# A two-layer perceiver on one core: projections of the recurrence in another order with key lengths by token, and experts that gather their tokens

## The chip, the core and the metric

One Trainium2 chip, and of it one core. The metric is the device time of one execution in microseconds, as the median of several runs. The kernel before takes 994.61 us (median of 3 runs, 992.96 to 995.33).

## What is computed

Sixteen batches of 64 rows of 256 numbers (1024 tokens in all) go through six parts, each added to its input: attention on a context, a gated recurrence, batch attention with a mixture of experts, attention on the context again, latent attention, and adapters. The change touches two of them.

```python
# recurrence: H = 16 heads of HD = 16, T = 64 steps, B = 16 batches
q = silu(x @ Wq); k = silu(x @ Wk); v = x @ Wv
log_f = log_sigmoid(x @ Wf1 @ Wf2); gamma = -sigmoid(x @ Wgamma)
k = k / max(norm(k, over the 16 numbers of a head), 1e-12)
a = k * gamma * exp(log_f)
S = S * exp(log_f)                      # at each step
S = S + k * (a . S + v);  o = q . S
...
# experts: 8 of them, room for C = 256 tokens each
logits = x @ wr                         # x normalized
top1, top2                              # two experts of each token
loc1 = cumsum(m1, axis=0) - 1;  loc2 = cumsum(m2, axis=0) - 1 + m1.sum(0)
buf[top1, s1] = x; buf[top2, s2] = x    # those beyond C are dropped
y = (relu(buf @ w1 + b1) @ w2 + b2) * 0.8
out = g1 * y[top1, s1] + g2 * y[top2, s2]
```

## The kernel before, in words

The program is a row of stages. Each is a block in which all engines run their own lists of instructions, tied by semaphores, and a stage begins when the one before has ended on all engines. A token is a column (transposed tiles, `[128, 2, 1024]`) or a row (`[128, 8, 256]`). The order of the work on every engine is written out by hand. In the trace TensorE (PE) splits each fp32 matmul into two passes, so a product over both halves of the 256 inputs shows as x4.

**Projections of the recurrence** (`recurrence_projections_stage`, tiles p_ and rec_; L237 to L385). Layer norm and transposes give `xnT`. Then for each half c of the columns (512 of them) PE goes through the thirteen jobs of `RJOBS`, each into one of four PSUM banks, which ScalarE (ACT) empties: k0 and k1 (the keys, two halves m of the 256 outputs), low (96 rows that feed the gates), q0, q1, g0, f0 (gamma and the forget gate from 16 rows of low), v0, v1, g1, f1, gate0, gate1. ACT takes k and q twice, as they are and through a sigmoid. VectorE (DVE) forms the keys (L260) and their squares (L262), PE sums the squares over each head with the matrix `same_head`, which gives every one of the 16 rows of a head the same sum (L357), ACT takes the roots of 512 columns (L385, another function table than that of the sigmoids), and DVE bounds them (L266), inverts them (L270), scales the keys (L274) and forms `a` (L279). GpSimd (POOL) multiplies gamma by f twice (L309, L312) and makes the queries (L315). All this is done for c = 0 and then for c = 1.

**Recurrence** (`recurrence_stage`, tiles r_; L570 to L735). For each of 64 steps and both halves m PE adds the values (L679) and the decayed state summed over a head (L683), DVE updates the state (L624, L628, L635), POOL fades it and multiplies it by the query (L656, L662), and PE sums the output (L690). The values of four steps are spread to a diagonal by 16 copies on ACT into a ring of four buffers (`value_rows`, L724); the first three rings are filled at the start of the stage, and the first matmul waits for the first.

**Experts** (`moe_stage`, tiles m_; L1689 to L1990). For each of eight tiles of 128 tokens: layer norm (DVE, L122 to L142), transposes (PE, L149), gain and shift (ACT, L159), logits (PE, L1860). Pairs of tiles g go through `choices` (DVE, L1745 to L1756: the two best experts and their one-hot rows), `counts` (PE, L1869) and `first_places` (DVE, L1767 on: the place of each token in the list of its expert). `rows_of` (L1760 to L1762) turns a place into a row number of the buffer `expert_rows` in DRAM, and POOL scatters the tokens to it by an indirect DMA: sixteen of 128 rows each, eight for the first choices and eight for the second, which need the totals of all first choices (L1839). The buffer was zeroed in the stage before (L1586, L1591). When all have landed, SyncE (SP) loads the 256 rows of each expert (L1969), PE turns them (`turn_rows`, L1884), ACT applies gain and shift (L1939), and PE runs the two layers (L1896, L1907) with DVE between them (L1818, L1828). While this goes on POOL scales the second bias (L1849) and adds two tiles (L1851). The weights of experts 2 to 7 stream in through SP.

```python
for c in range(2):
    for m in range(KD): squares(c, m)
    for m in range(KD): lengths(c, m)
    for m in range(KD): inverse_lengths(c, m)
    for m in range(KD): units(c, m)
    for m in range(KD): decays(c, m)
```

## Time and profile before

| | |
|---|---|
| median of 3 runs | 994.61 us |
| the profiled execution, its own time | 992.36 us |
| its span | 990.6 us |
| TensorE (PE) busy | 841.5 us, 85% |
| VectorE (DVE) busy | 589.6 us, 60% |
| ScalarE (ACT) busy | 430.1 us, 43% |
| GpSimd (POOL) busy | 339.4 us, 34% |

The profile is of one execution. Its times count from the start of the span. An engine is busy while it computes; a row of the timeline merges neighbouring instructions of one kind and gives their start, the time from the first to the last, the engine, the line, what is written from what, the shape and the count, and in brackets how long the engine had been idle and for what it had waited. Matmuls overlap, so their price is read from the distance of their starts.

### The profile page before, as it was taken

What the parts mean: (1) busy time and instruction counts of PE and PEld (TensorE: products, weight loads), DVE (VectorE), ACT (ScalarE), POOL (GpSimd) and SP (SyncE); (2) the same over time, 40 slices, a digit from 0 to 9 for tenths busy, and PEclk for the clock granted to TensorE, in tenths of its full rate; (3) what the DMA queues carried; (4) which work ended last, traced back from release to release, by engine and by line L of the source; (5) the groups of instructions that cost most, each with busy time, mean ns of one, the idle gap of its engine ahead of it and who ended that gap; (6) DMA issues with size and microseconds to landing.
All of it is one profiled execution on the core that took longest, in us unless ns stands there. A gap on an engine that the chain in (4) does not pass through costs nothing. (4 is left out here: it accounts for less than half of the span.)

```text
span 990.6 us, 19998 instructions
## 1 busy us (share of the span) xinstructions
PE 841.5 (85%) x7396; PEld 631.3 (64%) x7396; DVE 589.6 (60%) x1374; ACT 430.1 (43%) x1245; POOL 339.4 (34%) x466
## 2 busy tenths in 40 slices
PE   5999997975999999759685399994789996687998
PEld 4888885434999999635464288883567773464344
DVE  3555556376999999671857032233696775463751
ACT  3666564657644550135444000000476663663730
POOL 2112111046999999210332800003533331250000
PEclk9999999887999999768795599997599997798999
DMA  7113500000000000000200255534353200000001
GB/s 237 31 33 102 187 13 2 1 0 1 1 1 2 1 1 1 1 1 0 87 2 28 85 159 172 189 107 143 110 153 90 73 24 0 2 3 1 1 1 43
DMA packets 45284, 51.72 MB, mean 52 GB/s; under 512 B 7205, under 2 KB 40850, under 8 KB 45060
## 3 DMA queue, kind: packets, MB, share of 16 engines
q1 hardware_dynamic: 40644, 43.47, 13.9%
q0 software_dynamic: 1536, 4.08, 1.3%
q10 hardware_dynamic: 3008, 2.88, 0.8%
q8 instruction: 60, 0.98, 0.4%
q14 instruction: 36, 0.29, 0.1%
HBM read 43.20 MB, written 7.34 MB: 51 GB/s over the span
## 5 line engine op out<-in xcount | busy, mean ns | idle before, releaser
L656 POOL TENSOR_TENSOR r_faded<-r_state,rec_f 128x256 f32<-128x256 f32 x128 | 82.1, 642 | 17.5 <-DVE r_state L635 7.2
L683 PE MATMUL r_u_ps<-r_t_in,l_same_head 128*128 128x256 f32 x256 | 87.1, 422 | 0.2
L662 POOL TENSOR_TENSOR r_q_in<-r_state,rec_q 128x256 f32<-128x256 f32 x128 | 82.1, 641 | 0.3 <-DVE r_state L635 0.2
L690 PEld LDWEIGHTS r_o_ps<-l_head_of,r_q_in 128*128 128x128 f32 x512 | 77.3, 192 | 6.9 <-POOL r_q_in L662 0.4
L1360 ACT ACTIVATE a_prob<-a_s_ps,a_negmax 128x256 f32<-128x256 f32 x128 | 59.0, 488 | 41.2 <-DVE a_negmax L1397 41.2
L1020 ACT ACTIVATE a_prob<-a_s_ps,a_negmax 128x256 f32<-128x256 f32 x128 | 59.1, 486 | 19.7 <-DVE a_negmax L1076 19.7
L690 PE MATMUL r_o_ps<-l_head_of,r_q_in 128*128 128x8 f32 x512 | 65.4, 236 | 0.3 <-POOL r_q_in L662 0.3
L628 DVE TENSOR_TENSOR r_update<-r_u_ps,rec_k 128x256 f32<-128x256 f32 x128 | 55.2, 431 | 6.8 <-PE r_u_ps L683 6.8
L1896 PE MATMUL m_h_ps<-m_rowsT,l_w 128*128 128x256 f32 x256 | 58.2, 387 | 0.3 <-ACT m_rowsT L1939 0.3
L1818 DVE TENSOR_SCALAR m_hidden<-m_h_ps,l_b 128x256 f32<-128x256 f32 x64 | 28.0, 479 | 48.7 <-PE m_h_ps L1896 48.7
L635 DVE TENSOR_TENSOR r_state<-r_update,r_faded 128x256 f32<-128x256 f32 x128 | 54.3, 424 | 4.4
L624 DVE TENSOR_TENSOR r_t_in<-r_state,r_par_ps 128x256 f32<-128x256 f32 x128 | 53.7, 421 | 5.3
L1223 POOL DMA_INDIRECT a_got<-expert_out,all_slot x16 | 15.5, 969 | 118.1 <-DMA expert_out<-m_y 113.8
L1896 PEld LDWEIGHTS m_h_ps<-m_rowsT,l_w 128*128 128x128 f32 x256 | 49.8, 195 | 7.7 <-issue 0.7
L1082 DVE COPY a_probT<-a_w_ps 128x512 f32<-128x512 f32 x48 | 31.5, 687 | 39.0 <-PE a_w_ps L941 38.9
L1907 PE MATMUL m_y_ps<-l_w,m_hidden 128*128 128x256 f32 x240 | 53.9, 379 | 0.0
L1939 ACT ACTIVATE m_rowsT<-m_xt_ps,l_B_s,l_B_g 128x256 f32<-128x256 f32 x16 | 8.0, 560 | 103.5 <-PE m_xt_ps L1884 103.5
L1076 DVE TENSOR_REDUCE a_negmax<-a_s_ps 128x2 f32<-128x512 f32 x64 | 39.7, 683 | 17.6 <-PE a_s_ps L932 17.6
L1397 DVE TENSOR_REDUCE a_negmax<-a_s_ps 128x2 f32<-128x512 f32 x64 | 40.8, 681 | 15.3 <-PE a_s_ps L1287 14.5
L1907 PEld LDWEIGHTS m_y_ps<-l_w,m_hidden 128*128 128x128 f32 x240 | 45.1, 190 | 5.9
L1296 PE MATMUL a_w_ps<-all_ident,a_prob 128*128 128x128 f32 x256 | 41.6, 298 | 8.4 <-ACT a_prob L1360 3.3
L860 POOL TENSOR_TENSOR a_spread<-a_rden,all_half 128x256 f32<-128x256 f32 x16 | 9.8, 614 | 106.3 <-DVE a_rden L1088 106.3
(321 smaller groups left out, 1983.2 us busy)
## 6 DMA issues: line engine op xcount, KB each, us to landing
l_w<-in_B_w SPq DMA_DIRECT2D x16, 1024.0 KB, 6.0
a_ctxT<-in_ctxT SPq DMA_DIRECT2D x31, 256.0 KB, 2.8
a_ctx<-in_ctx SPq DMA_DIRECT2D x16, 256.0 KB, 3.2
expert_rows<-ffn_zeros SPq DMA_DIRECT2D x8, 256.0 KB, 2.9
m_rows<-expert_rows SPq DMA_DIRECT2D x8, 256.0 KB, 5.9
expert_out<-m_y ACTq DMA_DIRECT2D x7, 256.0 KB, 6.5
all_X<-in_x SPq DMA_DIRECT2D x4, 256.0 KB, 5.4
l_b<-in_B_b SPq DMA_DIRECT2D x1, 1024.0 KB
```

The source lines that it names most:

```text
L624: nc.vector.tensor_tensor(t_in[m][:, :, :], state[(t + 1) % 2][m][:, :, :], a, ALU.mult).then_inc(t_ready[m], 1)
L628: nc.vector.tensor_tensor(update[:, m, :, :], u_ps[t % 2][m][:, 0:B, :], row("k", t, m), ALU.mult).then_inc(upd_ready[m], 1)
L635: nc.vector.tensor_tensor(state[t % 2][m][:, :, :], update[:, m, :, :], faded[m][:, :, :], ALU.add).then_inc(state_ready[m], 1)
L656: nc.gpsimd.tensor_tensor(faded[m][:, :, :], state[(t + 1) % 2][m][:, :, :], row("f", t, m), ALU.mult).then_inc(faded_ready[m], 1)
L662: nc.gpsimd.tensor_tensor(q_in[t % 2][m][:, :, :], state[t % 2][m][:, :, :], row("q", t, m), ALU.mult).then_inc(q_ready[m], 1)
L683: nc.tensor.matmul(u_ps[t % 2][m][:, 0:B, :], same_head[:, :], t_in[m][:, :, :], start=False, stop=True).then_inc(u_mm[m], 1)
L690: mm = nc.tensor.matmul(o_ps[:, 2 * m + c, :, t % U], q_in[t % 2][m][:, c * (B // 2):(c + 1) * (B // 2), :], head_of[:, :], start=True, st ...
L1020: ins = nc.scalar.activation(prob[n % 2][:, r, m, :], s_ps[r][:, m, :], ACT.Exp, bias=negmax[n % 2][:, r, m:m + 1], accum_out=den[n % 2][: ...
L1296: mm = nc.tensor.transpose(acc[:, (2 * m + c) * P:(2 * m + c + 1) * P], prob[n % 2][:, r, m, c * P:(c + 1) * P], ident[:, :])
L1360: ins = nc.scalar.activation(prob[n % 2][:, r, m, :], s_ps[r][:, m, :], ACT.Exp, bias=negmax[n % 2][:, r, m:m + 1], accum_out=den[n % 2][: ...
L1896: mm = nc.tensor.matmul(h_ps[i][:, f, :], w1[j][:, k, (2 * i + f) * P:(2 * i + f + 1) * P], rowsT[j][:, k, :], start=(k == 0), stop=(k == ...
L1907: mm = nc.tensor.matmul(y_bank(e, slice(c, c + 1))[:, 0, :], hidden[j][:, f, c * P:(c + 1) * P], w2[j][:, f, :], start=(f == 0), stop=(f = ...
```

## The change

Three things are changed in the recurrence's first stage and one in the experts.

1. `RJOBS` is a list of pairs. Keys, low and queries of both halves of the columns come first, then all roots, then for each half gates, g, f and v. The values are taken by DVE instead of ACT.
2. Key lengths are summed by token: PE multiplies each 128 columns of squares (stationary) by `head_of` (`sums`), which gives 8 numbers per token; ACT takes 128x32 roots, DVE bounds and inverts 128x32, copies each number 16 times into `wide`, and PE turns `wide` back into columns by a product with the identity (`spread`); `units` reads that from PSUM. POOL squares f, and DVE multiplies `a` in two steps (`gated_units`, `decays`).
3. The value rows of the first four steps are made at the end of the projections, eight copies on ACT and eight on DVE, into QT; the recurrence makes only the later ones.
4. Experts: no buffer of rows in DRAM, no zeroing and no scatter. SP stores the normalized tiles to `routed_rows` as they come. DVE makes one-hot rows of place and of expert (`hot_rows`), PE multiplies them into a table that says for each row of each expert which token it holds (`tokens`), and POOL gathers the rows of each expert by two indirect DMAs (`gather_rows`). Layer norm of all tiles now stands ahead of all routing on DVE.

```diff
-RJOBS = ("k0", "k1", "low", "q0", "q1", "g0", "f0", "v0", "v1", "g1", "f1", "gate0", "gate1")
...
+RJOBS = [(c, name) for c in range(2) for name in ("k0", "k1", "low", "q0", "q1")] + [(c, name) for c in range(2) for name in ("gate0", "gate1", "g0", "f0", "g1", "f1", "v0", "v1")]
...
-                    nc.vector.tensor_scalar(r["k_sig"][:, m, cols(c)], r["k_sig"][:, m, cols(c)], 1e-12, None, ALU.max).then_inc(len_ready, 1)
-                def inverse_lengths(c, m):
+                    nc.vector.tensor_scalar(length[:, c, m, :, :], length[:, c, m, :, :], 1e-12, None, ALU.max).then_inc(len_ready, 1)
                     dve.wait_ge(len_ready, ONE + KD * c + m + 1)
-                    nc.vector.reciprocal(r["k_sig"][:, m, cols(c)], r["k_sig"][:, m, cols(c)]).then_inc(n_ready, 1)
+                    nc.vector.reciprocal(inverse[:, c, m, :, :], length[:, c, m, :, :]).then_inc(inv_ready, 1)
+                    dve.wait_ge(inv_ready, ONE + KD * c + m + 1)
+                    nc.vector.tensor_copy(wide[:, c, m, :, :, :], inverse[:, c, m, :, :].unsqueeze(3).to_broadcast([P, CH, HH, HD])).then_inc(n_ready, 1)
                 def units(c, m):
...
-                    dve.wait_ge(n_ready, ONE + KD * c + m + 1)
-                    nc.vector.tensor_tensor(r["k"][:, m, cols(c)], r["k"][:, m, cols(c)], r["k_sig"][:, m, cols(c)], ALU.mult).then_inc(unit_ready, 1)
+                    dve.wait_ge(spread_mm, ONE + KD * c + m + 1)
+                    nc.vector.tensor_tensor(r["k"][:, m, cols(c)], r["k"][:, m, cols(c)], n_ps[m][:, :], ALU.mult).then_inc(unit_ready, 1)
+                def gated_units(c, m):
+                    dve.wait_ge(unit_ready, ONE + KD * c + m + 1)
+                    wait_read(dve, c, f"g{m}")
+                    nc.vector.scalar_tensor_tensor(r["a"][:, m, cols(c)], r["k"][:, m, cols(c)], -1.0, r["gamma"][:, m, cols(c)], ALU.mult, ALU.mult).then_inc(part_ready, 1)
                 def decays(c, m):
-                    dve.wait_ge(unit_ready, ONE + KD * c + m + 1)
+                    dve.wait_ge(part_ready, ONE + KD * c + m + 1)
                     dve.wait_ge(twice_ready, ONE + KD * c + m + 1)
-                    nc.vector.scalar_tensor_tensor(r["a"][:, m, cols(c)], r["k"][:, m, cols(c)], -1.0, r["gamma"][:, m, cols(c)], ALU.mult, ALU.mult).then_inc(a_ready, 1)
+                    nc.vector.tensor_tensor(r["a"][:, m, cols(c)], r["a"][:, m, cols(c)], r["k_sig"][:, m, cols(c)], ALU.mult).then_inc(a_ready, 1)
+                def values(c, m):
+                    dve.wait_ge(acc_mm, ONE + RJOBS.index((c, f"v{m}")) + 1)
+                    nc.vector.tensor_copy(r["v"][:, m, cols(c)], acc[RJOBS.index((c, f"v{m}")) % RING][:, :]).then_inc(v_read, 1)
...
+                dve.wait_ge(v_read, ONE + 2 * KD)
+                for i in range(1, HD, 2):
+                    nc.vector.tensor_scalar(first_out(i), first_v, diag[:, i:i + 1], None, ALU.mult).then_inc(rows_ready, 1)
...
+                def queries(c, m):
+                    wait_read(pool, c, f"q{m}")
+                    nc.gpsimd.tensor_tensor(r["q"][:, m, cols(c)], r["q"][:, m, cols(c)], r["q_sig"][:, m, cols(c)], ALU.mult).then_inc(q_ready, 1)
+                def decays_twice(c, m):
+                    pool.wait_ge(k_done, ONE + KD * c + m + 1)
+                    wait_read(pool, c, f"f{m}")
+                    nc.gpsimd.tensor_tensor(r["k_sig"][:, m, cols(c)], r["f"][:, m, cols(c)], r["f"][:, m, cols(c)], ALU.mult).then_inc(twice_ready, 1)
...
+                def sums(c, m):
+                    pe.wait_ge(sq_ready, ONE + KD * c + m + 1)
+                    for j in range(CH):
+                        t = CH * c + j
+                        mm = nc.tensor.matmul(n_ps[m][:, (CH * c + j) * HH:(CH * c + j + 1) * HH], r["a"][:, m, t * P:(t + 1) * P], head_of[:, :], start=True, stop=True)
+                    mm.then_inc(n_mm, 1)
+                def spread(c, m):
+                    pe.wait_ge(n_ready, ONE + KD * c + m + 1)
+                    pe.wait_ge(n_taken, ONE + 2 * KD)
+                    if c >= 1:
+                        pe.wait_ge(unit_ready, ONE + KD * (c - 1) + m + 1)
+                    for j in range(CH):
+                        mm = nc.tensor.matmul(n_ps[m][:, j * P:(j + 1) * P], wide[:, c, m, j, :, :].rearrange("p h k -> p (h k)"), ident[:, :], start=True, stop=True)
+                    mm.then_inc(spread_mm, 1)
...
-                            nc.tensor.matmul(n_ps[m][:, :], same_head[:, :], r["a"][:, m, cols(c)], start=True, stop=True).then_inc(n_mm, 1)
+                            sums(c, int(name[1]))
+                for c in range(2):
+                    for name in ("gate0", "gate1", "g0", "f0", "g1", "f1", "v0", "v1"):
+                        product(c, name)
+                        if name == "f1":
+                            spread(c, 0)
+                            spread(c, 1)
...
+                def lengths(c, m):
+                    act.wait_ge(n_mm, ONE + 2 * KD)
+                    nc.scalar.activation(length[:, c, m, :, :], n_ps[m][:, CH * HH * c:CH * HH * (c + 1)].rearrange("p (j h) -> p j h", j=CH), ACT.Sqrt).then_inc(n_taken, 1)
...
+                    if (c, name) == (1, "q1"):
+                        for half in range(2):
+                            lengths(half, 0)
+                            lengths(half, 1)
+                act.wait_ge(v_read, ONE + 2 * KD)
+                for i in range(0, HD, 2):
+                    nc.scalar.activation(first_out(i), first_v, ACT.Copy, scale=diag[:, i:i + 1]).then_inc(rows_ready, 1)
...
-                    pe.wait_ge(v_ready, ONE + HD * (t // V + 1))
+                    if t >= V:
+                        pe.wait_ge(v_ready, ONE + HD * (t // V))
...
-                for n in range(3):
+                for n in range(1, 3):
...
-                def rows_of(ts, c):
-                    step.link(nc.vector.scalar_tensor_tensor(row[:, ts, c], chosen[:, ts, c], float(CAP), place[:, ts, c], ALU.mult, ALU.add))
+                def hot_rows(ts, c):
+                    n = ts.stop - ts.start
+                    nc.vector.tensor_scalar(upper[:, ts, c], place[:, ts, c], P + 0.5, float(P), ALU.is_gt, ALU.mult)
                     step.link(nc.vector.tensor_scalar(over[:, ts, c], place[:, ts, c], CAP + 0.5, 2.0 * ROWS, ALU.is_gt, ALU.mult))
-                    nc.vector.scalar_tensor_tensor(slot_kept[:, ts, c], row[:, ts, c], -1.0, over[:, ts, c], ALU.add, ALU.add).then_inc(kept_ready, 1)
+                    nc.vector.tensor_tensor(row[:, ts, c], place[:, ts, c], upper[:, ts, c], ALU.subtract)
+                    step.link(nc.vector.scalar_tensor_tensor(part_at[:, ts, c], chosen[:, ts, c], float(CAP), upper[:, ts, c], ALU.mult, ALU.add))
+                    nc.vector.tensor_tensor(over[:, ts, c], over[:, ts, c], part_at[:, ts, c], ALU.add)
+                    step.link(nc.vector.tensor_tensor(row_hot[:, ts, c, :], row[:, ts, c].unsqueeze(2).to_broadcast([P, n, P]), row_no.unsqueeze(1).to_broadcast([P, n, P]), ALU.is_equal))
+                    step.link(nc.vector.tensor_tensor(part_hot[:, ts, c, :], over[:, ts, c].unsqueeze(2).to_broadcast([P, n, PARTS]), part_no.unsqueeze(1).to_broadcast([P, n, PARTS]), ALU.is_equal))
+                    nc.vector.tensor_scalar(token_hot[:, ts, c, 0, :], part_hot[:, ts, c, :], place_no, None, ALU.mult)
+                    nc.vector.tensor_tensor(token_hot[:, ts, c, 1, :], part_hot[:, ts, c, :], tile_no[:, ts].unsqueeze(2).to_broadcast([P, n, PARTS]), ALU.mult).then_inc(hot_ready, 1)
...
-                    if g >= 2:
-                        choices(g - 2)
-                    if g >= 3:
-                        first_places(g - 3)
-                choices(3)
-                first_places(2)
-                first_places(3)
+                choices(0)
+                for g in range(1, NT // 2):
+                    choices(g)
+                    first_places(g - 1)
+                first_places(NT // 2 - 1)
...
+                dve.wait_ge(token_mm, ONE + 1)
+                step.link(nc.vector.tensor_reduce(token_sum[:, :], token_ps.rearrange("p i h -> p h i"), AX.X, ALU.add))
+                nc.vector.tensor_copy(token[:, :], token_sum[:, :]).then_inc(token_ready, 1)
...
-                def scatter(t, c):
-                    nc.gpsimd.indirect_dma_start(out=buf_d, out_offset=bass.IndirectOffsetOnAxis(ap=slot_kept[:, t, c:c + 1], axis=0), in_=xn[:, t, :], in_offset=None,
-                                                 bounds_check=ROWS - 1, oob_is_err=False).then_inc(scattered, 16)
-                pool.wait_ge(*cleared)
-                for t in range(NT):
-                    pool.wait_ge(kept_ready, ONE + t // 2 + 1)
-                    scatter(t, 0)
-                pool.wait_ge(kept_ready, ONE + NT // 2 + 1)
-                for t in range(NT):
-                    scatter(t, 1)
+                def gather_rows(e):
+                    if e >= 2:
+                        pool.wait_ge(xt_mm, ONE + e - 1)
+                    for c in range(2):
+                        nc.gpsimd.indirect_dma_start(out=rows[e % 2][:, c, :], out_offset=None, in_=xn_d, in_offset=bass.IndirectOffsetOnAxis(ap=token[:, 2 * e + c:2 * e + c + 1], axis=0)).then_inc(rows_in[e % 2], 16)
+                pool.wait_ge(stored, ONE + 16 * NT)
+                pool.wait_ge(token_ready, ONE + 1)
+                gather_rows(0)
+                gather_rows(1)
                 nc.gpsimd.tensor_scalar(b2[:, :, :], b2[:, :, :], 1.0 - DROPOUT, None, ALU.mult).then_inc(b2_ready, 1)
                 for t in range(NT):
                     nc.gpsimd.tensor_tensor(X[:, t, :], X[:, t, :], Y[:, t, :], ALU.add).then_inc(x_summed, 1)
+                for e in range(2, E):
+                    gather_rows(e)
             @block.tensor
...
+                def tokens(ts, c):
+                    pe.wait_ge(hot_ready, ONE + (ts.stop // 2 if c == 0 else NT // 2 + 1))
+                    for t in range(ts.start, ts.stop):
+                        mm = nc.tensor.matmul(token_ps, row_hot[:, t, c, :], token_hot[:, t, c, :, :], start=(c == 0 and t == 0), stop=(c == 1 and t == NT - 1))
+                    if c == 1:
+                        mm.then_inc(token_mm, 1)
...
-                sp.wait_ge(scattered, 16 * 2 * NT)
-                load_rows(0)
-                load_rows(1)
-                load_rows(2)
+                for t in range(NT):
+                    sp.wait_ge(normed.scaled, ONE + t + 1)
+                    sp.dma_start(xn_d[t * P:(t + 1) * P, :], xn[:, t, :]).then_inc(stored, 16)
                 load_first(2)
-                load_rows(3)
                 load_first(3)
                 for e in range(2, E):
                     load_second(e)
```

On ACT, in the projections of c = 0, the order was this (names: rec_ are the results, p_acc the banks, p_n_ps the sums of squares):

```order
L377 ACTIVATE rec_q<-p_acc 128x512
L377 ACTIVATE rec_q_sig<-p_acc 128x512
L377 ACTIVATE rec_gamma<-p_acc 128x512
L377 ACTIVATE rec_f<-p_acc 128x512
L385 ACT_TABLE_LOAD
L385 ACTIVATE rec_k_sig<-p_n_ps 128x512 x2
L377 ACTIVATE rec_v<-p_acc 128x512 x2
L377 ACT_TABLE_LOAD
L377 ACTIVATE rec_gamma<-p_acc 128x512
```

The changed kernel has, once for both halves:

```order
L426 ACTIVATE rec_q<-p_acc 128x512
L426 ACTIVATE rec_q_sig<-p_acc 128x512
L434 ACT_TABLE_LOAD
L434 ACTIVATE p_length<-p_n_ps 128x32 x4
L429 ACT_TABLE_LOAD
L429 ACTIVATE rec_gate<-p_acc 128x512 x2
L426 ACTIVATE rec_gamma<-p_acc 128x512
L426 ACTIVATE rec_f<-p_acc 128x512
```

Two of four loads of a table are gone, and the roots stand in one place. On PE the same stretch of the changed kernel, from the first sums on, reads:

```order
L385 MATMUL p_n_ps<-l_head_of,rec_a 128x8 x4
L365 MATMUL p_acc<-all_xnT,l_R_Wq 128x512 x2
L385 MATMUL p_n_ps<-l_head_of,rec_a 128x8 x4
L377 MATMUL p_acc<-l_R_up,rec_low 128x256 x4
L372 MATMUL p_acc<-rec_low,l_R_up 128x512 x4
L395 MATMUL p_n_ps<-all_ident,p_wide 128x128 x8
L365 MATMUL p_acc<-all_xnT,l_R_Wv 128x512 x4
L377 MATMUL p_acc<-l_R_up,rec_low 128x256 x4
```

The eight products with the identity (x8) are new, and all products from 16 rows (L377, L372) of a half stand together. On POOL, from batch attention through the experts, the kernel before and the changed one:

```order
L1591 MEMSET ffn_zeros 128x512
L1595 TENSOR_TENSOR a_prob<-a_prob,a_rden 128x512 x16
L1509 UNCONDITIONAL_BRANCH
L1836 UNCONDITIONAL_BRANCH
L1839 DMA expert_rows<-ffn_xn,ffn_slot_kept 2048x256 x16
L1849 TENSOR_SCALAR l_b<-l_b 128x2048
L1851 TENSOR_TENSOR all_X<-all_X,ffn_Y 128x256 x8
```

```order
L1651 TENSOR_TENSOR a_prob<-a_prob,a_rden 128x512 x16
L1577 UNCONDITIONAL_BRANCH
L1909 UNCONDITIONAL_BRANCH
L1915 DMA m_rows<-routed_rows,m_token 128x256 x4
L1921 TENSOR_SCALAR l_b<-l_b 128x2048
L1923 TENSOR_TENSOR all_X<-all_X,ffn_Y 128x256 x8
L1915 DMA m_rows<-routed_rows,m_token 128x256 x12
```

Four indirect DMAs instead of sixteen stand ahead of the first expert; twelve more stand behind POOL's other work.

## Rows read from the trace of the kernel before

**Rows 1.** Windows, projections and experts: PE, PEld, DVE, ACT, POOL busy, PE clock, DMA.
```profile
170.00:228.00 58.00, 43.13 (x112) 19.29 (x112) 35.80 (x52) 31.48 (x57) 16.64 (x12) 0.81 0.00 1
521.60:680.00 158.40, 129.26 (x636) 113.51 (x636) 52.02 (x180) 18.38 (x40) 26.64 (x25) 0.86 0.36 118
```
**Rows 2.** Timeline, DVE and ACT at the end of the projections.
```profile
213.68 1.28 ACT L385 ACT_TABLE_LOAD   x1
214.97 1.09 ACT L385 ACTIVATE rec_k_sig<-p_n_ps 128x512 f32<-128x512 f32 x2
...
216.43 6.56 DVE L270 RECIPROCAL rec_k_sig<-rec_k_sig 128x512 f32<-128x512 f32 x2
...
222.91 2.53 DVE L274 TENSOR_TENSOR rec_k<-rec_k,rec_k_sig 128x512 f32<-128x512 f32 x2
```
**Rows 3.** Timeline, PE in the projections.
```profile
187.43 1.88 PE L330 MATMUL p_acc<-all_xnT,l_R_Wq 128*128 128x512 f32 x4
189.14 1.02 PE L357 MATMUL p_n_ps<-rec_a,l_same_head 128*128 128x512 f32 x2
190.09 1.13 PE L337 MATMUL p_acc<-rec_low,l_R_up 16*128 16x512 f32 x4
191.15 3.70 PE L330 MATMUL p_acc<-all_xnT,l_R_Wv 128*128 128x512 f32 x8
...
197.77 5.37 PE L330 MATMUL p_acc<-all_xnT,l_R_Wk 128*128 128x512 f32 x8 [0.50 <-ACT rec_gamma L377]
```
**Rows 4.** Window of the second half's first products, columns as in rows 1.
```profile
198.00:202.50 4.50, 4.50 (x7) 1.76 (x7) 4.50 (x4) 2.18 (x5) 4.31 (x4) 0.62 0.00 0
```
**Rows 5.** Timeline of weight loads, steady state of the recurrence.
```profile
299.88 0.63 PEld L690 LDWEIGHTS r_o_ps<-l_head_of,r_q_in 128*128 128x128 f32 x4
300.43 0.30 PEld L683 LDWEIGHTS r_u_ps<-r_t_in,l_same_head 128*128 128x128 f32 x2
```
**Rows 6.** One line of DVE: min/median/max of its durations, ns.
```profile
L279 DVE SCALAR_TENSOR_TENSOR rec_a<-rec_k,rec_gamma x4: 679/1212/1745, 204.1 to 227.0; 128x512 f32<-128x512 f32 x4
```
**Rows 7.** Timeline, start of the recurrence.
```profile
228.32 4.87 ACT L724 ACTIVATE rec_gamma<-rec_v,l_diag 128x128 f32<-128x128 f32 x16
...
233.24 2.07 PE L679 MATMUL r_u_ps<-rec_gamma,l_same_head 128*128 128x256 f32 x4 [14.65 <-ACT rec_gamma L724]
...
236.21 0.43 DVE L628 TENSOR_TENSOR r_update<-r_u_ps,rec_k 128x256 f32<-128x256 f32 x1 [6.77 <-PE r_u_ps L683]
```
**Rows 8.** Timeline, DVE routing in the experts' stage.
```profile
523.68 0.71 DVE L142 TENSOR_SCALAR ffn_xn<-ffn_Y,m_x_meanvar,m_x_rstd 128x256 f32<-128x256 f32 x2
...
525.18 0.70 DVE L142 TENSOR_SCALAR ffn_xn<-ffn_Y,m_x_meanvar,m_x_rstd 128x256 f32<-128x256 f32 x2
...
536.42 0.17 DVE L1745 COPY m_logits<-m_h_ps 128x16 f32<-128x16 f32 x1 [1.11 <-PE m_h_ps L1860]
...
537.83 0.18 DVE L1767 TENSOR_TENSOR m_count<-m_h_ps,m_onehot 128x32 f32<-128x32 f32 x1
538.27 0.16 DVE L1760 SCALAR_TENSOR_TENSOR m_row<-m_chosen,m_place 128x2 f32<-128x2 f32 x1
...
543.47 0.17 DVE L1762 SCALAR_TENSOR_TENSOR ffn_slot_kept<-m_row,m_over 128x8 uint32<-128x8 f32 x1
```
**Rows 9.** Timeline, from the last scatter to the experts.
```profile
556.29 0.97 POOL L1839 DMA_INDIRECT expert_rows<-ffn_xn,ffn_slot_kept  x1 [0.31 <-issue]
557.29 5.41 POOL L1849 TENSOR_SCALAR l_b<-l_b 128x2048 f32<-128x2048 f32 x1
...
561.52 1.97 PE L1884 MATMUL m_xt_ps<-all_ident,m_rows 128*128 128x128 f32 x8 [20.11 <-DMA m_rows<-expert_rows]
...
562.64 5.49 POOL L1851 TENSOR_TENSOR all_X<-all_X,ffn_Y 128x256 f32<-128x256 f32 x8
...
563.84 15.75 PE L1896 MATMUL m_h_ps<-m_rowsT,l_w 128*128 128x256 f32 x64 [0.35 <-ACT m_rowsT L1939]
```
**Rows 10.** The gathers of the stage after the experts (a_got).
```profile
DMA to landing us min/median/max: 2.8/3.8/5.7
```

More of the change, by code:

```diff
@@ L1919, in _ @@
                 totals()
+                for g in range(NT // 2):
+                    tokens(slice(2 * g, 2 * g + 2), 0)
+                tokens(slice(0, NT), 1)
                 turn_rows(0)
```

173 lines of the change are left out of this document (84 added, 89 removed).

## The prediction

> **What bounds the kernel now.** The windows by stage come first [rows 1]. In the 58 us of the projections PE is busy for 43.1 and DVE for 35.8, and in the 158.4 us of the experts PE for 129.3: neither stage is full on any engine, so both must be read at the places where every engine waits for one. The timeline shows three. At the end of the projections [rows 2] PE and ACT are done, and DVE still inverts 2 x 512 columns (6.56 us), scales the keys (2.53) and forms `a`; the last of these starts at 227.0 and takes 0.68 [rows 6], so the stage ends at 227.7. At the start of the recurrence [rows 7] PE waits until 233.24 for ACT's 16 copies (4.87 us). In the experts [rows 9] PE stands still for 20.11 us before the first expert; what ends it is a chain: sixteen scatters at a distance of 1.28 us on POOL, the last from 556.29, their landing, the load of the rows. From 563.84 on PE is full. The recurrence itself and everything behind the experts are not touched.
>
> **Projections.** The two halves no longer alternate. PE has finished the sums of c = 0 at 190.09, since a sum takes 0.95 us there (189.14 to 190.09 [rows 3]). What follows now is k, k, low, q, q of the second half instead of gates and values, 1.71 us each (187.43 to 189.14), and two sums. A sum is now eight passes of 128 columns by 8. The nearest row is the recurrence's output, which loads the same 128x128 weights: four passes in 0.55 us (299.88 to 300.43 [rows 5]), 0.14 each, and 0.11 when PE's other passes are subtracted. Eight of them cost 0.9 to 1.1 us, so nothing is won or lost against 0.95. That gives 190.1 + 8.6 + 1.9 = 200.6. ACT then empties the last queries (two copies of 0.55 [rows 2], until 201), loads a table (1.28 [rows 2]), takes four roots of 128x32 (no row has the shape; half of 0.55 at most, at least 0.15: I take 0.2), loads the other table (1.28), and reads gate0 (0.5): 204.9. PE meanwhile makes gate0, gate1, g0 and f0; four passes from 16 rows take 1.06 us (190.09 to 191.15), which I take for each gate and for each pair of g and f, so it is done at 203.8 and waits 1.1 us for a bank. Then g1, f1 (1.06): 206.0. The first `spread` is ready long before that, since DVE bounds, inverts and copies in about 1.1 us (two small instructions at 0.2 each [rows 8] and one of 512 at 0.68 [rows 6]). Each is eight passes of 128 columns, bounded by 0.11 (weight load) and 0.14 a pass: 0.9 to 1.1, and two cost 1.9. Values 3.4: 211.3. The second half repeats this without a wait: 2.1 + 2.1 + 1.9 + 3.4 = 9.5, to 220.8.
>
> That holds at full clock. In the row of windows behind the first stretch of 16-row products the granted clock is 0.62 [rows 4], a mix of the two levels (1.2 and 2.4 GHz), and the eight passes from 197.77 take 5.37 us instead of the 3.7 of the same work from 191.15 [rows 3]: 1.7 us lost per stretch. The changed order makes two such stretches, both longer (4 us against 2.5), each with `spread` and values behind it. I charge 1.7 twice: PE ends at 224.2. Bounds: nothing, and twice as much.
>
> Behind the last value DVE copies it (0.68), finishes `a` (two products at 0.68 [rows 6]) and makes eight value rows of 128 elements (0.2 each by the small rows [rows 8]); ACT's eight take 8 x 4.87 / 16 = 2.43 us [rows 7], beside that. Together about 3.5 us: **the stage ends at 227.7, as before, 0 us**, with ends at 224 (full clock) and 231. So the reciprocals, 13 us of DVE, leave the path, and PE takes their place.
>
> A product of two SBUF tiles on DVE takes 0.68 us alone and 1.75 beside POOL (minimum and maximum of one shape [rows 6]); this is also why the scaling of the keys takes 2.53 for two [rows 2]. The queries that caused it now run early. POOL's squares of f stand beside `units`, which reads PSUM. I count the late products at 0.68; if they collided again it would be 1.1 us for each half, inside the bounds. The Trainium skill (SBUF — State Buffer, section "SBUF: two separate sides") says that a VectorE instruction with two SBUF inputs and a GpSimd one exclude each other for a whole instruction; by that rule `units` is free and only `gated_units` and `decays` can wait, so it gives the same sum within 1.1 us.
>
> ACT's next function starts 1.29 us after a load began (213.68 to 214.97 [rows 2]), so a switch costs the 1.28 of its row. The Trainium skill (ScalarE: Activation LUTs, section "What ACT_TABLE_LOAD costs") puts a drain of about 1.38 us on top of each load. The trace shows none; by the page the two loads that stand between the last query and gate0 would hold PE 2.8 us longer, and the gain would be smaller by that.
>
> **Recurrence.** Its first matmul no longer waits for ACT. It started 5.2 us into the stage (228.0 to 233.24 [rows 7]); now it can start at once, and the decayed sums behind it need the cleared state and the parameters, on other engines and within a us of the start. The second ring is wanted at step 4, ten us later, and takes 4.87. **-5.1 us**. Bounds: -4 and -6.
>
> **Experts.** Layer norm now stands ahead of the routing on DVE: scaling of pairs starts at 523.68 and 525.18, 1.5 us apart [rows 8], so the fourth is done at 523.68 + 4.5 + 0.7 = 528.9. Then comes routing, bound by DVE. `choices` takes 1.4 us (536.42 to 537.83), with its last cast not linked. `first_places` had two linked steps of 0.22 and three small ones; now it has two and nine, of which four are not waited for (0.1 each), four are (0.2), and one writes 256 elements (0.4, from 0.68 for 512): 2.1 us. Four of each: 14.0, plus 0.8 once, since the logits of tiles 2 and 3 come about that late. The part for second choices: 0.7 for the totals, then nine steps on 8 tiles, one of them of 1024 elements (1.3), together 3.1. Tokens on PE and back through DVE: 1.1. Sum: 528.9 + 14.0 + 0.8 + 3.1 + 1.1 = 547.9. Routing was over at 543.64 before [rows 8], so this part is 4.3 us later. But then four indirect DMAs stand between the end of routing and PE, where eleven did (543.5 to 556.29 at 0.97 + 0.31 us): POOL starts about 1 us after its data, at 548.9, and the fourth at 548.9 + 3 x 1.28 = 552.7. A gather of the next stage lands in 2.8 us at least and 3.8 in the median [rows 10], there beside other traffic; here the queues are empty and I take 2.8: 555.5. PE turns the second expert's rows (half of 1.97 [rows 9]) and starts the first layer at 556.5 instead of 563.84: -7.3. The low clock after the pause is then met by products instead of turning, 0.9 us back. **-6.4 us**. Bounds: -9 (steps on DVE at 0.1) and -2.5 (landing 5.7, the 1024 elements at twice the price).
>
> Behind that POOL does the bias (5.41) and eight sums (5.49) and then gathers for expert 2: 553.7 + 10.9 + 2.3 + at most 5.7 = 572.6. PE wants these rows after 64 products (15.75 us) and half of the second layer, 576 at the earliest: hidden. The later gathers have a whole expert's time. Stores of tiles by SP run beside layer norm. The zeroing before stood beside attention and cost nothing; the table's load is one small DMA among many.
>
> **Sum.** 0 - 5.1 - 6.4 = -11.5 us. The profiled execution took 992.36, which gives 980.9; it stands 2.25 below the median of the runs, so against that median I say **983.1 us**. A difference of 0.2% (2 us) is about what a measurement of this kernel can tell from none.
>
> **The rivals.** (a) *The clock holds in the projections*: no loss behind the 16-row stretches, the stage ends at 224.2, 3.5 us earlier: 979.6. For it: the stretch at 190.09 was followed by values at full rate [rows 3]. Against it: [rows 4]. (b) *Gathers land late*: fp32 rows from DRAM at 3.8 to 5.7 us, and expert 2 waits behind POOL's sums: 1 to 4 us back, 984 to 987. (c) *DVE is the bound of routing by more*: the comparison against 128 numbers costs twice as much in both shapes (4 x 0.4 + 1.3 = 2.9 us), and half of the layer norm that moved ahead delays routing by 3: 989. (d) *Slower*: PE stays at its lower level from 200.6 to the end of the projections. Its 18 us of work there become 36, the stage ends at about 242, 14.5 us later than in my sum: 997.6. It decides from the point where the granted clock, once down behind the first stretch, has not come back before the second begins, 9 us later; [rows 4] is for it with its 0.62, and against it is that the loss there was 1.7 us and not more. [...] (e) *The change doesn't do what it says*: the sum by token costs as much as it spares, if each of its 64 passes takes what a 16-row pass takes (1.06 / 4 = 0.27 [rows 3]) instead of 0.12: 9.3 us more, and with the 1.1 of a collision on DVE 993.5, no difference.
>
> **How the numbers follow.** Forecast as summed, with ends 979 to 987: 0.55. (a) 0.17, (b) 0.12, (c) 0.08, (d) 0.04, (e) 0.04. The range leaves out (d), (e) and the tails of (a) and (c): 975 to 988.5. Faster by over 0.2%: 0.92; within: 0.04; slower: 0.04.
>
> **What would show it.** Right: two reciprocal rows of 3.3 us gone, PE's last value near 224 and the stage's end near 228; first update of the recurrence about 3 us into its stage; four gathers from about 549, PE's first layer near 556.5. Wrong: a stage end past 231, PE waiting for `m_rows` again at expert 2, routing over after 551, or a time above 990.

## The result, and the profile after

The changed kernel takes **982.02 us** (median of 4 runs, 979.65 to 984.38) against 994.97 for the kernel before beside it (4 runs, 992.96 to 997.25): ratio 0.9874, 95% interval 0.9847 to 0.9901. The profiled execution took 982.78 us, its span is 981.0. The forecast was 983.1, its range 975 to 988.5.

The windows by stage, columns as in [rows 1], which they answer to:

```profile
170.00:227.50 57.50, 48.08 (x168) 27.86 (x168) 27.18 (x72) 27.65 (x58) 9.20 (x8) 0.85 0.00 1
515.90:674.30 158.40, 130.70 (x652) 114.42 (x652) 60.56 (x218) 19.77 (x41) 31.04 (x30) 0.87 0.39 124
```

In the projections DVE is down from 35.8 to 27.2 us of work and PE is up from 43.1 to 48.1; POOL's share is nearly halved. PE's timeline there, which answers to [rows 3]:

```profile
187.88 0.95 PE L385 MATMUL p_n_ps<-l_head_of,rec_a 128*128 128x8 f32 x8
188.69 3.68 PE L365 MATMUL p_acc<-all_xnT,l_R_Wk 128*128 128x512 f32 x8
...
199.13 1.34 PE L377 MATMUL p_acc<-l_R_up,rec_low 16*128 16x256 f32 x5
...
203.27 2.56 PE L372 MATMUL p_acc<-rec_low,l_R_up 16*128 16x512 f32 x4 [2.04 <-ACT rec_gate L429]
205.76 3.78 PE L395 MATMUL p_n_ps<-all_ident,p_wide 128*128 128x128 f32 x16
209.33 3.77 PE L365 MATMUL p_acc<-all_xnT,l_R_Wv 128*128 128x512 f32 x8
213.04 1.34 PE L377 MATMUL p_acc<-l_R_up,rec_low 16*128 16x256 f32 x5
...
216.96 3.45 PE L395 MATMUL p_n_ps<-all_ident,p_wide 128*128 128x128 f32 x16
220.25 3.60 PE L365 MATMUL p_acc<-all_xnT,l_R_Wv 128*128 128x512 f32 x8
```

A sum takes 0.81 us (187.88 to 188.69), each half pays for one stretch at a low clock (spread 3.78 and 3.45 us), and PE stands for 2.04 us ahead of g1, waiting for ACT to read gate0. ACT in that pause, and the start of the recurrence, which answers to [rows 7]:

```profile
199.55 1.28 ACT L434 ACT_TABLE_LOAD   x1
200.85 0.46 ACT L434 ACTIVATE p_length<-p_n_ps 128x32 f32<-128x32 f32 x4
201.33 1.28 ACT L429 ACT_TABLE_LOAD   x1
202.62 1.08 ACT L429 ACTIVATE rec_gate<-p_acc 128x512 f32<-128x512 f32 x2
...
224.61 2.59 ACT L451 ACTIVATE all_QT<-rec_v,l_diag 128x128 f32<-128x128 f32 x8 [6.95 <-DVE rec_v L302]
```
```profile
225.69 1.70 DVE L332 TENSOR_SCALAR all_QT<-rec_v,l_diag 128x128 f32<-128x128 f32 x8
...
230.65 0.43 DVE L695 TENSOR_TENSOR r_update<-r_u_ps,rec_k 128x256 f32<-128x256 f32 x1 [1.52 <-PE r_u_ps L751]
```

The stage ends at 227.4, where DVE's eight rows end, and the first update stands at 230.65 (before 236.21), 3.3 us behind. In the experts the chain of [rows 9] is now this (POOL and PE):

```profile
541.85 1.17 POOL L1915 DMA_INDIRECT m_rows<-routed_rows,m_token  x1 [36.00 <-DVE m_token L1871]
...
545.83 0.95 POOL L1915 DMA_INDIRECT m_rows<-routed_rows,m_token  x1 [0.30 <-issue]
...
548.69 1.11 PE L1965 MATMUL m_xt_ps<-all_ident,m_rows 128*128 128x128 f32 x4 [1.52 <-DMA m_rows<-routed_rows,m_token]
...
549.60 10.75 PE L1977 MATMUL m_h_ps<-m_rowsT,l_w 128*128 128x256 f32 x38
```

The stage begins at 515.93 and the first layer at 549.60, 33.7 us later; before it was 42.0 (521.83 to 563.84). For expert 2 and later PE never waits for `m_rows`; its waits for them are two, 5.5 and 1.5 us at the first two experts.

**Where 4 us seem to go back.** PE's last product of the experts comes 13.6 us earlier than before (661.68, 675.30), and the span is only 9.6 us shorter. The difference arises in the second context attention, in which no instruction is changed. It took 124.0 us before (from PE's first turn at 693.74 to the last output product at 817.74) and 128.5 now. Its first 30 us, before and changed, are these windows:

```profile
693.70:723.70 30.00, 24.53 (x248) 17.92 (x248) 19.98 (x42) 15.11 (x54) 17.76 (x22) 0.66 0.36 109
```
```profile
679.70:709.70 30.00, 24.21 (x180) 16.68 (x184) 15.84 (x32) 14.01 (x49) 16.51 (x20) 0.56 0.32 91
```

The granted clock is 0.66 in one and 0.56 in the other. Whether the change does this or the execution is a question to the runs (changed_again).

### The profile page after: what moved, and what is told of

The parts are those of the page before. It is cut to its first block and busy times, and to the rows that moved or that the text cites. A ratio compares the mean times of both kernels' runs of the same rounds, so it can differ in the third digit from the quotient of the medians.

```text
span 981.0 us, 20166 instructions
## 1 busy us (share of the span) xinstructions
PE 851.5 (87%) x7468; PEld 642.9 (66%) x7468; DVE 586.8 (60%) x1426; ACT 421.9 (43%) x1231; POOL 330.2 (34%) x461
## 3 DMA queue, kind: packets, MB, share of 16 engines
q1 hardware_dynamic: 37588, 40.41, 13.2%
## 5 line engine op out<-in xcount | busy, mean ns | idle before, releaser
L758 PE MATMUL r_o_ps<-l_head_of,r_q_in 128*128 128x8 f32 x512 | 65.2, 236 | 0.3 <-POOL r_q_in L729 0.3
L1651 POOL TENSOR_TENSOR a_prob<-a_prob,a_rden 128x512 f32<-128x512 f32 x32 | 32.4, 1042 | 84.6 <-DVE a_rden L1712 84.6
L702 DVE TENSOR_TENSOR r_state<-r_update,r_faded 128x256 f32<-128x256 f32 x128 | 54.3, 424 | 4.4
```

Of the source, the lines that this page charges most:

```text
L702: nc.vector.tensor_tensor(state[t % 2][m][:, :, :], update[:, m, :, :], faded[m][:, :, :], ALU.add).then_inc(state_ready[m], 1)
L758: mm = nc.tensor.matmul(o_ps[:, 2 * m + c, :, t % U], q_in[t % 2][m][:, c * (B // 2):(c + 1) * (B // 2), :], head_of[:, :], start=True, st ...
```

## The experiments

"Stage" is the time from the table load that opens the projections to the first update of the recurrence (it holds the first three points of the change), "experts" that from the table load that opens their stage to the first layer, both in the profiled execution. Chips and calls differ by some us, so the ratio to the kernel before beside it counts.

| kernel | median us | before beside it | ratio (95%) | stage | experts |
|---|---|---|---|---|---|
| before | | | 1 | 66.1 | 42.0 |
| changed | 982.02 | 994.97 | 0.9874 (0.9847 to 0.9901) | 60.6 | 33.7 |
| experts_only | 986.36 | 994.65 | 0.9914 (0.9890 to 0.9938) | 65.2 | 33.5 |
| proj_only | 990.81 | 994.65 | 0.9954 (0.9930 to 0.9978) | 61.1 | 42.0 |
| rows_back | 986.73 | 994.65 | 0.9917 (0.9887 to 0.9947) | 64.3 | 33.7 |
| values_first | 978.87 | 994.65 | 0.9848 (0.9808 to 0.9889) | 57.8 | 33.6 |
| filled_pause | 983.30 | 993.90 | 0.9908 (0.9881 to 0.9936) | 57.6 | 33.6 |
| wide_inverse | 990.07 | 993.90 | 0.9961 (0.9939 to 0.9983) | 69.4 | 33.3 |
| one_hot_once | 978.45 | 993.90 | 0.9851 (0.9816 to 0.9886) | 60.9 | 31.0 |
| both | 975.19 | 993.90 | 0.9829 (0.9797 to 0.9861) | 57.5 | 31.0 |
| changed_again | 978.65 | 991.56 | 0.9871 (0.9848 to 0.9893) | 60.6 | 33.5 |
| filled_half | 975.43 | 991.56 | 0.9843 (0.9823 to 0.9863) | 59.3 | 33.3 |
| interleaved | 970.17 | 991.56 | 0.9789 (0.9772 to 0.9807) | 53.3 | 33.6 |
| interleaved_once | 968.13 | 991.56 | 0.9755 (0.9731 to 0.9779) | 54.0 | 31.0 |

**The parts by themselves.** experts_only and proj_only are the kernel before with the diff's part for `moe_stage` or for the two recurrence stages.

> The kernel before with only the experts' part of the change. Theory (the parts are independent and add up): the routing ends later within its stage, yet the first layer starts 33.6 us into the stage as in the changed kernel (before: 42.0), and nothing of that is given back by the experts behind it, so 8 us less than the kernel before: about 987, range 985 to 989. Rival (the experts' gain is given back later, as the changed kernel's profile with only 9.6 us less in its span could suggest): the first layer is 8 us earlier all the same, but the time is 990 or more.

> The kernel before with only the projections' part and the first value rows. Theory (parts add up): first update of the recurrence at about 230.6 (before 236.2), 5.5 us less than the kernel before, about 989.4, range 987.5 to 991; experts as before. Rival (the projections' gain reaches the end only together with the experts' part): 993 or more.

8.3 and 3.8 us less by the medians; their sum, 12.1, is what the whole change gave (12.95) within the intervals. By the traces it is 8.5 and 5.0. Both rivals fall, proj_only's by little: 990.8 against "993 or more", and its ratio's interval times 994.65 is 987.7 to 992.5. Each part carries its gain to the end alone.

**The first value rows.** rows_back deletes the sixteen rows at the end of the projections:

```diff
-                    nc.vector.tensor_scalar(first_out(i), first_v, diag[:, i:i + 1], None, ALU.mult).then_inc(rows_ready, 1)
...
-                for n in range(1, 3):
+                for n in range(3):
                     value_rows(n)
```

> The changed kernel, with the first ring of value rows made in the recurrence again. Theory: in the changed kernel ACT's eight rows and DVE's eight stand at the end of the projections, behind the last decayed product, and cost 1.6 us there; taken out, the stage ends 1.6 us earlier, and the recurrence starts with a wait of 5.2 us for 16 rows on ACT. Net 3.6 us more than the changed kernel, 985.6, range 984 to 987.5. Rival 1 (the rows are the whole gain of this part, the order of the projections gives nothing): 5.5 us more, 987.5. Rival 2 (the recurrence makes up for a late start): no difference, 982.

The stage is 3.7 us longer than the changed kernel's (64.3, 60.6), 3.6 expected; the time 0.43% longer by the ratios, 4.3 us. The recurrence starts with the row of the kernel before (ACT):

```profile
227.03 4.87 ACT L785 ACTIVATE all_QT<-rec_v,l_diag 128x128 f32<-128x128 f32 x16
```

So of the 5.5 us of these two stages 3.7 come with the rows, and 1.8 with the projections; of these 1.8, 0.9 is a loss to the clock in the profiled execution of the kernel before (its stage takes 66.1 us, that of experts_only with the same instructions 65.2).

**Inverting by token.** wide_inverse keeps the new order and inverts 512 columns again:

```diff
-                    nc.vector.tensor_copy(wide[:, c, m, :, :, :], inverse[:, c, m, :, :].unsqueeze(3).to_broadcast([P, CH, HH, HD])).then_inc(n_ready, 1)
+                    nc.vector.reciprocal(wide[:, c, m, :, :, :], length[:, c, m, :, :].unsqueeze(3).to_broadcast([P, CH, HH, HD])).then_inc(n_ready, 1)
```

> The changed kernel, in which DVE inverts the length of every one of 512 columns again (a reciprocal of 512 elements, 3.28 us, in place of the copy of 0.35 to 0.43), so that only the order of the products is new. Theory (inverting by token is what lets the order pay, since DVE's chain of lengths stands on the path): the four wide reciprocals end at about 215 on DVE, units of the first half only then, PE waits for banks in the second half, the stage ends about 8 us later, time about 990, range 987 to 993. Rival (the new order alone would have hidden the reciprocals, since they begin at 201 and the last is wanted at 217): first spread at 208 instead of 206, stage end 2 us later, time about 984.

990.07, stage 8.8 us longer. DVE's last reciprocal and first scaling, and PE's stop for a bank in the second half:

```profile
216.82 3.35 DVE L284 RECIPROCAL p_wide<-p_length 128x512 f32<-128x512 f32 x1
220.09 1.22 DVE L288 TENSOR_TENSOR rec_k<-rec_k,p_n_ps 128x512 f32<-128x512 f32 x2
```
```profile
223.16 4.37 PE L372 MATMUL p_acc<-rec_low,l_R_up 16*128 16x512 f32 x8 [2.33 <-DVE rec_v L302]
```

The stage is even 3.3 us longer than before the change (69.4, 66.1), although it has the value rows at the end of the projections: with the wide inverse the new order loses. It pays because an inverse of 128x32 takes 0.35 us. The run is not the order alone, as was expected of it: it keeps the sums by token and `spread` on PE, and the old sums in the new order were not run. Part of its 8.8 us is the clock, too, which is low for longer than in the changed kernel (6.8 us, below):

```profile
206.00:216.00 10.00, 7.96 (x22) 5.31 (x23) 9.86 (x7) 2.64 (x6) 2.08 (x2) 0.50 0.01 2
```

**The clock in the projections.** Four kernels ask what brings the two drops: values_first (both values ahead of the gates), filled_pause and filled_half (eight and four products that nothing reads, in PE's pause) and interleaved (v0 ahead of the gates, v1 between f0 and g1; DVE reads the values in that order).

```diff
-("gate0", "gate1", "g0", "f0", "g1", "f1", "v0", "v1")
+("v0", "v1", "gate0", "gate1", "g0", "f0", "g1", "f1")
```
```diff
+                        if (c, name) == (0, "g1"):
+                            for _ in range(8):
+                                nc.tensor.matmul(normed.turned_ps[0][:, 0:KD, :], ident[:, :], xnT[:, 0, 0:KD * P], start=True, stop=True)
                         product(c, name)
```
```diff
-("gate0", "gate1", "g0", "f0", "g1", "f1", "v0", "v1")
+("v0", "gate0", "gate1", "g0", "f0", "v1", "g1", "f1")
```

> The changed kernel with each half's two value products ahead of its gates, read by DVE ahead of the first inverse lengths, and the value rows ahead of the second half's products on DVE. The pause of 2.04 us in which PE waits for gate0 is then filled. Two theories of the low clock (0.50 from 203.3 to about 208 and 0.52 to 0.63 from 216 to 220 in the changed kernel). Theory 1 (the pause brings the first drop, and recurring pauses the second): no drop, each half takes about 8.5 us on PE, last spread over at about 216.5, stage end 7 us earlier, time about 975. Theory 2 (the drop follows the products from 16 rows and the spread passes, pause or not): the granted clock falls again behind each half's 16-row products, each half takes 10.5 to 11 us, last spread over at about 221, time about 979. Rival: DVE reads the values late and PE waits for their banks, no gain.

> The changed kernel with eight products of 128x256 (nothing reads them; 1.7 us at full clock) in PE's pause of 2.04 us ahead of the first half's g1. It adds work and takes none away. Theory 1 (the pause brings the first drop of the clock): the granted clock stays at 1.0 through g1, f1 and the first spread, these take 1.1 + 1.85 us instead of 2.56 + 3.78, the second half starts 3 us earlier, time about 979. Theory 2 (the narrow products bring the drop): the granted clock is at 0.5 behind 203 all the same, the first half as long as in the changed kernel, time 982.

> As filled_pause, but four products of 128x256 (filled_pause's eight took 3.7 us, 0.46 each, so four take 1.85), which fit in the pause of 2.04. Theory 1 (the pause is what the first drop needs): granted clock 1.0 through the first half, stage from its start to the first update 60.6 - 3.2 = 57.4 if the second drop stays away too as it did in filled_pause, 59 if it comes back. Theory 3 (it is not the pause, but the length of the stretch in which PE does 16-row products and spread passes with nothing wide between them): the four wide products in the middle of it also keep the clock up. Theory 2 (narrow products alone, whatever stands between): drop as in the changed kernel, 60.6. This run and interleaved together tell 1 from 3.

> The changed kernel with each half in the order v0, gate0, gate1, g0, f0, v1, g1, f1, spread. No pause on PE, as in values_first, but the 16-row products are broken by a wide one: 2.1 us, then v1 (1.7), then 1.1 and the spread (1.9). Theory 3 (an unbroken narrow stretch, of 5.6 us in values_first, brings the drop): granted clock 1.0 to the end of the last spread, projections' start to first update 57.8 - 3.5 = 54.3, time 975 to 976 (values_first less 3). Theory 2 (the narrow products bring it, broken or not): drop in both halves, 57.8, time as values_first, 978.9.

Windows of the changed kernel: one in PE's pause, where the first drop begins, then over the first drop and the second:

```profile
202.00:203.00 1.00, 0.00 (x0) 0.00 (x0) 0.93 (x5) 0.99 (x2) 0.00 (x0) 0.93 0.00 0
203.00:204.00 1.00, 0.73 (x2) 0.73 (x4) 0.93 (x5) 1.00 (x3) 0.00 (x0) 0.50 0.00 0
...
203.30:208.30 5.00, 5.00 (x16) 3.50 (x17) 1.95 (x6) 2.47 (x5) 2.08 (x2) 0.50 0.00 0
216.90:220.20 3.30, 3.30 (x17) 3.24 (x17) 0.69 (x1) 0.77 (x2) 1.95 (x2) 0.54 0.00 0
```

The first drop comes before g1 starts (203.27): ahead of it stand 2.1 us of 16-row products and 1.6 us of the pause. The level is low from 202.9 to 209.7 and from 216.5 to 220.0.

values_first, from its first 16-row product to the end of its spread, in two windows, with PE busy throughout:

```profile
202.70:206.50 3.80, 3.80 (x17) 2.04 (x16) 3.40 (x11) 2.31 (x6) 0.00 (x0) 0.99 0.00 0
206.50:210.00 3.50, 3.50 (x18) 3.50 (x18) 0.69 (x1) 0.86 (x2) 2.04 (x2) 0.52 0.02 5
```

The pause is gone and the clock falls all the same, in both halves: theory 1 falls, and the time is theory 2's (979 expected, 978.87). Then filled_pause, whose stage begins 2.9 us later in its execution: the first row holds the last gate products and the eight added ones, the second g1, f1 and the first spread, the third the end of the second half's 16-row products and its spread:

```profile
203.30:208.30 5.00, 5.00 (x27) 3.80 (x28) 3.58 (x12) 4.59 (x10) 1.04 (x2) 1.00 0.02 3
208.00:211.00 3.00, 3.00 (x21) 2.18 (x21) 0.86 (x2) 1.08 (x2) 1.59 (x2) 1.00 0.03 5
...
216.90:220.20 3.30, 3.30 (x21) 2.23 (x20) 0.69 (x1) 2.22 (x5) 1.92 (x2) 1.00 0.00 0
```

No drop in either half, which speaks against theory 2. Theory 3 was made from the two. filled_half (stage 59.3, 59 expected with the second drop back) keeps the first drop away and has the second back, in the half that nothing breaks up (first row from g1 on, second row spread and what is around it):

```profile
203.30:208.30 5.00, 4.88 (x25) 3.06 (x25) 3.54 (x11) 3.13 (x7) 2.04 (x2) 1.00 0.01 3
214.00:220.00 6.00, 6.00 (x20) 4.11 (x19) 1.50 (x3) 1.69 (x4) 2.08 (x2) 0.50 0.00 0
```

And interleaved has a wide product inside the narrow ones in both halves, a pause of only 0.22 us, and no drop to the end of the last spread:

```profile
205.00:208.00 3.00, 3.00 (x20) 2.08 (x20) 2.28 (x4) 1.08 (x2) 1.30 (x2) 1.00 0.00 0
...
211.00:214.90 3.90, 3.90 (x17) 1.46 (x15) 1.89 (x4) 2.17 (x4) 1.04 (x1) 1.00 0.02 4
214.90:217.00 2.10, 2.08 (x18) 1.86 (x16) 2.06 (x9) 1.97 (x6) 0.74 (x1) 1.00 0.00 0
```

Its stage takes 53.3 us, 7.3 less than the changed kernel's (54.3 expected), and its time is 8.5 us less beside it (970.17, 978.65; 975 to 976 expected, in a call in which the kernel before was 3 us faster as well). It and values_first have the same products and next to no pause; they differ in whether a wide product stands among the 16-row ones (and with it in the order in which DVE reads the values), and in the clock. That is what theory 3 says. The other kernels with these two orders agree: the kernel named both, with the order of values_first, is at 0.50 from 209 to 212 and from 220 to 222, and interleaved_once at 1.00 to the end of its last spread.

**Two things stay open.** In filled_pause the second half is not broken up, does 5.6 us of narrow products and spreads (214.54 to 220.15), and kept its clock, while filled_half lost it in the same products. So an unbroken narrow stretch does not always bring the drop, and no run here settles what else decides. And filled_pause's time (983.30, about 979 expected) does not show the 3.0 us by which its stage is shorter. Its profiled execution, which is also its median one, lost 2.9 us ahead of the projections, which begin at 172.96 instead of 170.06 (the granted clock from 20 to 60 us is 0.87 there, 0.91 in the changed kernel), and its second context attention took 128.8 us, the longest of all. That accounts for this execution; whether the other four had the same isn't known.

**The one-hot rows in one piece.** one_hot_once takes `hot_rows` out of `first_places` and calls it once for both choices of all tiles:

```diff
-                    hot_rows(ts, 0)
...
-                hot_rows(every, 1)
+                hot_rows(every, slice(0, 2))
```

> The changed kernel with the comparisons against 128 row numbers made once for all 16 choices of the 8 tiles, behind the totals, instead of four times for first choices and once for second ones. Theory (DVE bounds the routing, by the number of its small linked instructions): four groups of nine instructions of 1.55 us go, the last group grows by about 1.8 us, PE's sum has 16 products behind it instead of 8 (0.4), and the logits of the later tiles, which come from 522 to 529.5, now hold DVE for 1 to 2 us: token numbers 2.5 us earlier, first layer 2.5 us earlier, time about 979.5, range 978 to 981. Rival (PE's logits and counts bound the routing once DVE has less to do): token numbers as early as before or later, 982 to 983.

The experts' first layer comes 2.7 us earlier in its stage (31.0, 33.7), the time 0.23% by the ratios. DVE's comparison and the casts behind it:

```profile
535.50 2.28 DVE L1834 TENSOR_TENSOR m_row_hot<-m_row,l_route 128x2048 bf16<-128x2048 f32 x1
...
539.90 0.17 DVE L1873 CAST m_token<-m_token_sum 128x16 uint32<-128x16 f32 x1
```

Five comparisons, four of 0.42 us and one of 1.22 (2.9 together), became one of 2.28; the rest of the gain is four times eight small instructions that are no longer issued, less the waits for logits and counts that DVE now has between the groups (0.74, 0.87, 0.62 and 0.42 us in the kernel named both).

**Together, and once more.**

> values_first and one_hot_once together. Theory: the two gains add: the difference of values_first to the changed kernel plus 2.5 us, 976.5 by theory 2 of the clock and 972.5 by theory 1. Rival (what is gained before the recurrence or the experts is lost in later stages by another phase of the clock): the stages in question are shorter by as much, but the time is within 1 us of the better of the two.

> The changed kernel once more, beside the others of this call. It gives the changed kernel's time from more executions and a second look at where its clock falls. Theory (where the level changes in the stages ahead of and behind the changed ones differs from execution to execution, by up to 3 us ahead of the projections and 4.8 us in the second context attention, as the profiles of the eight kernels so far show with the same instructions there): median 981 to 984, projections' start to first update 60.6 us within 0.6, experts' start to first layer 33.6 within 0.2, second context attention anywhere from 124 to 129. Rival (the second context attention is longer because of the change): 128 to 129 again in the attention.

> interleaved and one_hot_once together: the best version so far, if interleaved's gain is there. Expected: first layer 31.0 us into the experts as in one_hot_once, projections' start to first update as in interleaved, so interleaved less 2.6 us: 972.5 by theory 3, 975.2 (as the run named both) by theory 2.

both is 0.19% below values_first by the ratios, and its experts 2.5 us shorter. changed_again has the changed kernel's instructions in the second context attention, and takes 124.7 us there (680.33 to 805.08) where the first profile took 128.5. Its first 30 us:

```profile
680.30:710.30 30.00, 24.54 (x246) 17.95 (x247) 19.67 (x41) 15.14 (x54) 17.72 (x22) 0.65 0.36 109
```

0.65, as before the change (0.66). Over all fourteen profiles this attention takes 121.1 to 128.8 us with one and the same code. So the 4 us that the changed kernel's profile seems to give back belong to that execution, not to the change, and the medians are what counts: the changed kernel stands 12.95 us below the kernel before in its first call and 12.91 in this one (ratios 0.9874 and 0.9871). The same holds for single kernels: interleaved's profile has the shortest of these attentions. **interleaved_once is the fastest kernel here**: 968.13, 10.5 us below the changed kernel beside it and 23.4 below the kernel before (972.5 was expected of it).

## Why the prediction was right

**Projections, 0 us.** Right in the sum (stage end 227.4, forecast 227.7; PE's last value ends at 223.85, forecast 224.2), from terms that were off and cancelled, which is luck. The sums took 0.81 instead of 0.95, and the first keys had a higher clock than in the profile before, so PE reached the 16-row products at 199.13, not 200.6. The gates took 0.97 for both, not 1.06 each. But ACT read gate0 3.5 us behind that point, so the pause was 2.04 instead of 1.1. The term that was mis-sized is the charge for the low clock, 1.7 a stretch: by the same products at full clock (filled_pause for the second half, interleaved for g1, f1 and spread) the first drop cost 1.4 on g1 and f1, 1.7 on spread and 0.2 on the values (3.7 us for eight, 3.5 in filled_pause), 3.3; the second 1.6. Together 4.9 instead of 3.4, and PE's start 1.5 us earlier paid for it. [rows 4] gave the right sign and the price of the second stretch; the first one was low for 6.8 us, the second for 3.4.

The spread at full clock is 1.89 (209.12 to 211.01 in filled_pause; 1.9 charged). DVE's late products took 1.28 for two, with POOL idle beside them: 0.68 was right. What POOL did hold up, in interleaved_once, is a copy that the forecast had no collision for (last section). The table loads were followed by the next function after 1.30 and 1.29 us; the drain that the Trainium skill (ScalarE: Activation LUTs, section "What ACT_TABLE_LOAD costs") puts on top is not in this trace either.

**Recurrence, -5.1.** The first matmul starts as soon as the stage does, the first update is 3.3 us in: right. The rows' own price, 1.6 us at the end of the projections, was in the tail of 3.5 (measured 3.5, from the last value at 223.88 on DVE to 227.39, the rows 1.7 of it); rows_back shows both sides of it.

**Experts, -6.4.** Mechanism right, size short by 1.3: first layer 33.7 us into the stage against 34.7 forecast, and 0.6 us instead of 0.9 lost to the clock behind it (last product 112.1 us after the first layer, 111.5 before). `choices` 1.4, `first_places` 2.0 (2.1 forecast), second choices 3.4 (3.1), tokens 0.9 (1.1), four gathers at a distance of 1.25 to 1.48 us, and a landing of 2.86 (2.8). Most of the us of difference is in the start, where scaling was done 0.7 us earlier than taken; the wait of 0.8 for later logits was 0.7, and four `choices` and four `first_places` took 13.7 instead of 14.0.

**Rivals.** (a) The clock didn't hold; interleaved shows that it could, and that this was worth more than the 3.5 us that were put on it. (b) The second gather for expert 2 was issued at 559.1; with 2.9 to land it stood some 7 us ahead of PE, whose turning of these rows lets POOL go on at 570.1. (c) The comparison cost what was taken, 0.42 and 1.22. (d) The clock came back both times, after 6.8 and after 3.4 us. (e) A pass of the sum took 0.10 us.

**Sum.** In the traces -5.5 and -7.7 make -13.2 (forecast -11.5), the medians -12.95. The 0.9 us that the kernel before lost to the clock in its first keys is in the first number and belongs to its profiled execution: experts_only, with the old projections, has a stage of 65.2. Against that the first number would be -4.6, half a us from the forecast of -5.1.

## What to carry to other kernels

When a slow stretch of one engine is moved under another's work, look at what the other engine then does in a row: here the same products in another order were worth 7.3 us, 2.8 with the pause filled (values_first) and 4.5 more with one wide product among the narrow ones (interleaved), which is more than the 5.5 us that the change itself gave there. What is said of the wide product comes from a few orders of one kernel, and one half (filled_pause) does not fit it. Price a path of many small linked instructions by their number, since merging five groups into one saved 2.7 us although the same elements were compared. And do not read a loss behind a change from one profile: an untouched stage of 125 us differed by up to 7.7 us between executions.

## What the runs showed of the hardware

- PE can be busy without a gap and still lose its clock: in values_first, at 16-row products and 128-column passes with their weight loads, it fell to 0.5 (1.2 GHz) in both halves. The Trainium skill (TensorE: Matmul & The Clock Gate, section "HAM oscillation — how this bites in real kernels") tells of pauses as the cause; these rows show a case without one.
- A weight load of 128x128 with 8 columns behind it costs 0.10 us a pass (0.81 for eight), and with 128 columns 0.12 (1.89 for sixteen). At the low clock the latter is 0.22 (3.57 for sixteen).
- A product of 128x256 in fp32 takes 0.46 us (3.65 for eight), two passes of 0.23; filled_pause was sized with 0.21 a product and overfilled the pause by 1.6 us.
- DVE's copy of 512 elements from SBUF to SBUF takes 0.43 us alone, and 1.08 where POOL multiplies beside it (interleaved_once):

```profile
205.84 0.43 DVE L284 COPY p_wide<-p_inverse 128x512 f32<-128x512 f32 x1
...
206.78 1.08 DVE L284 COPY p_wide<-p_inverse 128x512 f32<-128x512 f32 x1
```
